# LoRA's output product one step later and in a bank of its own, and layer 1's k and v written as one 16-bit pair

## The reference, cut to what matters

```
x = x + tanh(g_xattn[0]) * L0_xattn(layernorm(x), ctx)   # 32 heads, 8 kv heads of 128, rms-normed q and k
x = x + tanh(g_ffn[0])   * L0_ffn(layernorm(x))          # LoRA experts behind a softmax router
x = x + tanh(g_xattn[1]) * L1_xattn(layernorm(x), ctx)   # 16 heads, 4 kv heads of 96, no norm of q and k
x = x + tanh(g_ffn[1])   * L1_ffn(layernorm(x))          # gated, 1792 wide

# L0_ffn
scores = H * softmax(x @ Wr.T + br)
low = einsum('bsd,hrd->bshr', x, A)
out = einsum('bshr,hor,bsh->bso', low, B, scores)        # H=8, r=16: 128 ranks
```

## Time and profile before

| | |
|---|---|
| median of 3 runs | 1188.02 us (1186.46 to 1189.14) |
| the profiled execution's own time | 1189.01 us |
| its span, first to last instruction | 1187.2 us |
| PE busy | 1129.7 us, 95% of the span |
| DVE busy | 844.7 us, 71% |
| ACT busy | 836.9 us, 70% |
| POOL busy | 374.2 us, 32% |
| mean granted clock of PE | 0.990 |

### The profile page before, as it was taken

One profiled execution on the slowest core, in us unless ns is written; L12 is line 12 of the kernel. 1 busy time (PEld: TensorE's weight loads), 2 busy tenths in 40 slices (PEclk: granted clock), 3 DMA queues, 4 the chain that ended last, 5 costly groups with the idle time before them and its releaser, 6 DMA issues.

```text
span 1187.2 us, 22719 instructions
## 1 busy us (share of the span) xinstructions
PE 1129.7 (95%) x7184; PEld 712.0 (60%) x7184; DVE 844.7 (71%) x2050; ACT 836.9 (70%) x2711; POOL 374.2 (32%) x685
## 2 busy tenths in 40 slices
PE   6789999999999999999999978799999999799998
PEld 4445666666666666666666645566676766455554
DVE  5578767767767767777677678988888888743434
ACT  5678878888888888878888677777777665522221
POOL 5554434334733333333343354321111121000000
PEclk9899999999999999999999999999999999999999
DMA  6465554464655545555545646758996796200000
GB/s 242 105 143 120 130 130 103 120 139 89 133 144 128 118 99 130 125 112 129 122 98 112 135 93 135 146 132 173 229 193 142 139 166 126 52 1 1 36 1 36
DMA packets 411991, 139.55 MB, mean 118 GB/s; under 512 B 386656, under 2 KB 396640, under 8 KB 411872
## 3 DMA queue, kind: packets, MB, share of 16 engines
q1 hardware_dynamic: 409968, 134.43, 51.2%
q0 software_dynamic: 1904, 3.67, 1.1%
HBM read 39.21 MB, written 2.10 MB: 35 GB/s over the span
## 4 chain that ended last, share of the span: by engine, by line
PE 79%; DVE 9%; ACT 5%; issue 3%; POOL 2%; DMA 1%; DVEq 0%; POOLq 0%; ACTq 0%
PE bank L519 22%; PE bank L520 22%; PE bank L521 22%; PE bank L720 8%; PE bank L739 4%; ACT probs L906 2%; DVE pieces L1084 2%; DVE stats L1095 1%; DVE mx L1185 1%; DVE x L1222 1%; ACT junk L811 1%; POOL rstd L1473 1%; DVE q_rows L1084 0%; DVE nb L1195 0%; DVE nb L1190 0%
## 5 line engine op out<-in xcount | busy, mean ns | idle before, releaser
L808 ACT ACTIVATE pieces<-probs,rs 128x256 f16<-128x256 f32 x384 | 166.3, 524 | 10.2 <-DVE rs L1202 9.4
L1185 DVE TENSOR_REDUCE mx<-bank 128x2 f32<-128x512 f32 x192 | 131.5, 685 | 56.8 <-PE bank L521 56.7
L1084 DVE SCALAR_TENSOR_TENSOR pieces<-probs,rs,pieces 128x256 f16<-128x256 f32 x384 | 163.3, 485 | 5.8 <-ACT pieces L808 5.0
L906 ACT ACTIVATE probs<-bank,nb,rq 128x256 f32<-128x256 f32 x256 | 141.1, 564 | 37.2 <-DVE nb L1190 36.9
L519 PE MATMUL bank<-wq,xT 128*128 128x512 f16 (+1 forms) x384 | 139.1, 362 | 2.7 <-DVE wq L1084 2.7
L519 PE MATMUL bank<-wo_hi,oT 128*128 128x512 f16 x352 | 133.4, 379 | 6.0 <-DVE oT L1084 4.6
L520 PE MATMUL bank<-wq,xT 128*128 128x512 f16 (+1 forms) x384 | 138.9, 362 | 0.0
L521 PE MATMUL bank<-wq,xT 128*128 128x512 f16 (+1 forms) x384 | 138.7, 361 | 0.0
L811 ACT ACTIVATE junk<-bank 128x128 bf16<-128x128 f32 x384 | 101.7, 289 | 52.0 <-PE bank L521 51.8
L521 PE MATMUL bank<-wo_hi,oT 128*128 128x512 f16 x352 | 133.4, 379 | 0.0
L520 PE MATMUL bank<-wo_lo,oT 128*128 128x512 f16 x352 | 133.4, 379 | 0.0
(11 more groups left out here) (187 smaller groups left out, 2651.2 us busy)
## 6 DMA issues: line engine op xcount, KB each, us to landing
raw_o<-in_wo_a SPq DMA_DIRECT2D x8, 1024.0 KB, 5.8
raw_q<-in_wq_a SPq DMA_DIRECT2D x7, 1024.0 KB, 5.9
raw_kv<-in_wkv_a SPq DMA_DIRECT2D x8, 512.0 KB, 3.8
turned<-pieces SPq DMA_TRANSPOSE x192, 2.8
raw_q<-in_wq_c SPq DMA_DIRECT2D x4, 768.0 KB, 5.0
raw_o<-in_wo_c SPq DMA_DIRECT2D x4, 768.0 KB, 5.1
down_rest<-in_down_t POOLq DMA_DIRECT2D x5, 512.0 KB, 4.3
ff_in<-in_gate_t SPq DMA_DIRECT2D x4, 448.0 KB, 4.0
```

The lines of the kernel that those rows point to most:

```text
L808: return act.activation(out, in_, ACT.Copy, scale=scale)
L906: act.activation(probs[:, h, :], bank[h // 2][:, (h % 2) * KV:(h % 2 + 1) * KV], ACT.Exp, bias=nb[:, h:h + 1], scale=scale, accum_out=sums ...
L1084: return dve.scalar_tensor_tensor(out, in_, scale, hi, ALU.mult, ALU.subtract)
L1185: dve.tensor_reduce(mx[:, pr], chunks(bank[i][:, :], 2), AX.X, ALU.max, negate=True).then_inc(mx_done, 1)
```

## The change

- LoRA's output product of tile t leaves step 59+t and stands in step 60+t behind the kv projection, in bank 3. PE's waits for `lora_added` ahead of the sums go; the product itself waits for the previous tile's.
- `lora_add` and the statistics of norm 2 go to the start of the next DVE step, behind `o_low`. In these steps the low pieces of the weights (`weight_low`) also go there, ahead of `lora_add`.
- Norm 2 is scaled by DVE (`norm_scale`, between the two row maxima) and copied to 16 bits by POOL, where ACT wrote both. POOL makes its rstd behind norm 1's rows, and no shift.
- In layer 1 ACT writes k and v as one 16-bit pair `kvp` (192 columns for each source) and DVE its low pieces; kn and POOL's k_pieces go, and k's transfer reads `kvp`. In layer 0 k_pieces writes into `kvp`.
- nb is a tensor_tensor in layer 0 and a tensor_scalar in layer 1. The tile `zeros`, its memset and a tile for `k_rows` go, `junk` shares memory with the feed-forward's hT, and one POOL wait is added at step 85.

```diff
-        v = [tuple(chunks(w, 2) for w in pair(f"v{i}", 2 * P)) for i in range(VS)]
+        kvp = [sb(f"kvp{i}", 8 * P, F16)[:, :].rearrange("p (j n d) -> p j n d", j=2, n=4) for i in range(VS)]
...
+        def kv_pair(n, c, i):
+            return kvp[n % VS][:, 1, 2 * c + i, :] if n < N0 else kvp[n % VS][:, :, 2 * c + i, 0:L1.hd]
...
+        def kv_source(n, i):
+            if n < N0:
+                return kv_bank(n)[:, i * L0.kvw + L0.hd:(i + 1) * L0.kvw]
+            return chunks(kv_bank(n)[:, i * L1.kvw:(i + 1) * L1.kvw], 2)
...
+        def low_late(n):
+            return beside(n + 1)[3] is not None
...
             def turn_k(n):
-                sp.wait_ge(klo_done, n + 1)
+                if n < N0:
+                    sp.wait_ge(klo_done, n + 1)
+                else:
+                    sp.wait_ge(vlo_done, 2 * n + 2)
                 if n >= 2:
                     sp.wait_ge(s_done, 2 * (n - 1))
-                sp.dma_start_transpose(k_half[n % 2], k_rows[:, :]).then_inc(kturned, 16)
+                if n >= 1:
+                    sp.wait_ge(kturned, 16 * n)
+                sp.dma_start_transpose(k_half[n % 2], kvp[n % VS][:, 0].rearrange("p n d -> p (n d)")).then_inc(kturned, 16)
...
             def lora_project_out(t):
                 pe.wait_ge(lora_lo, t + 1)
-                mm3(bank[2][:, :], tT[t % 2], lb, start=True, stop=True).then_inc(lora_out, 1)
+                if t >= 1:
+                    pe.wait_ge(lora_added, t)
+                mm3(bank[3][:, :], tT[t % 2], lb, start=True, stop=True).then_inc(lora_out, 1)
...
                 if T < N:
                     kv_proj(T)
-                if lora is not None and lora >= 1:
-                    pe.wait_ge(lora_added, lora)
-                if n == N0 + 3:
-                    pe.wait_ge(lora_added, NT)
+                if norm2 is not None:
+                    lora_project_out(norm2)
                 sums_of_step(n)
...
                 values(n)
-                if lora is not None:
-                    lora_project_out(lora)
...
-                    copy(v[n % VS][0][:, i, 0:L.hd], kv_bank(n)[:, i * L.kvw + L.hd:(i + 1) * L.kvw],
-                         alpha[:, i, c:c + 1]).then_inc(vhi_done, 1)
+                    copy(kv_pair(n, 0, i), kv_source(n, i), alpha[:, i, c:c + 1]).then_inc(vhi_done, 1)
...
-                if norm2 is not None:
-                    norm_scaled(2, norm2)
...
-                    dve.scalar_tensor_tensor(nb[:, pr], mx[:, pr], 1.0, rq[:, c:c + 2], ALU.mult, ALU.mult
-                                             ).then_inc(nb_done, 1)
+                    dve.tensor_tensor(nb[:, pr], mx[:, pr], rq[:, c:c + 2], ALU.mult).then_inc(nb_done, 1)
...
-                    dve.scalar_tensor_tensor(nb[:, pr], mx[:, pr], es[:, g % 2, s:s + 1], zeros[:, :], ALU.mult, ALU.add
-                                             ).then_inc(nb_done, 1)
+                    dve.tensor_scalar(nb[:, pr], mx[:, pr], es[:, g % 2, s:s + 1], None, ALU.mult).then_inc(nb_done, 1)
...
                 if n >= 1:
                     o_low(n - 1)
+                if n >= 1 and low_late(n - 1):
+                    for chunk in weight_chunks(n - 1):
+                        weight_low(*chunk)
+                if norm2 is not None:
+                    lora_add(norm2)
+                    norm_stats(2, norm2)
...
                 if S < N:
                     row_max(S, 0)
+                if norm2 is not None:
+                    norm_scale(2, norm2)
...
                 if T < N:
                     v_low(T)
+                if T < N0:
                     k_rows_scaled(T)
...
-                for chunk in weight_chunks(n):
-                    weight_low(*chunk)
-                if lora is not None:
-                    lora_add(lora)
-                    norm_stats(2, lora)
+                if not low_late(n):
+                    for chunk in weight_chunks(n):
+                        weight_low(*chunk)
...
-                if k in (1, 2):
+                if k == 1:
                     pool.wait_ge(norm[k].rstd, t + 1)
...
-                if k == 0:
+                if k in (0, 2):
                     pool.tensor_copy(rows[:, 0:D], xn[xn_slot(k, t)]).then_inc(norm[k].row_hi, 1)
...
-                if norm2 is not None:
-                    norm_rstd(2, norm2)
...
                 if norm2 is not None:
+                    norm_rstd(2, norm2)
                     norm_rows(2, norm2)
...
-                if T < N:
+                if T < N0:
                     k_pieces(T)
```

More of the change, by code:

```diff
@@ L189, in build @@
         xt = chunks(sb("x", NT * D)[:, :], NT)
-        junk = sb("junk", 6 * P, BF16)
         k_weight, q_weight = sb("k_weight", P)[:, :], sb("q_weight", P)[:, :]
         lora_act = [sb(f"lora_act{i}", P)[:, :] for i in range(2)]
+        junk = nc.alloc_sbuf_tensor_at("junk", [P, 6 * P], BF16, offset=(nc.sbuf_base + 31) // 32 * 32)
         hT = [tuple(sb(f"hT{i}_{w}", D, F32R)[:, :] for w in ("hi", "lo")) for i in range(2)]
@@ L241, in norm_bank, with v_piece, k_piece @@
             return bank[2 if k == 0 and t == 0 else 4 if k == 3 and t >= NT - 2 else 3]
+        def kv_pair(n, c, i):
+            return kvp[n % VS][:, 1, 2 * c + i, :] if n < N0 else kvp[n % VS][:, :, 2 * c + i, 0:L1.hd]
+        def v_piece(n, c, i):
+            return kvp[n % VS][:, 1, 2 * c + i, 0:layer_of(n).hd]
+        def k_piece(n, c):
+            return kvp[n % VS][:, 0, 2 * c:2 * c + 2, :]
+        def kv_source(n, i):
+            if n < N0:
+                return kv_bank(n)[:, i * L0.kvw + L0.hd:(i + 1) * L0.kvw]
+            return chunks(kv_bank(n)[:, i * L1.kvw:(i + 1) * L1.kvw], 2)
         def kv_bank(n):
@@ L551, in kv_proj @@
                 if n >= 2 and first:
-                    pe.wait_ge(kn_done, 2 * (n - 1) if n <= 4 else 2 * n)
+                    pe.wait_ge(kn_done if n <= N0 else vlo_done, 2 * (n - 1) if n <= 4 else 2 * n)
                 if t == 0 and first:
@@ L609, in values @@
                 for kt in range(2):
-                    last = mm3(bank[4][0:L.hd, :], [w[:, kt, 0:L.hd] for w in v[n % VS]],
+                    last = mm3(bank[4][0:L.hd, :], [v_piece(n, c, kt) for c in range(2)],
                                [turned_out[:, n % 2, c, kt] for c in range(2)], start=kt == 0, stop=kt == 1)
@@ L876, in v_hi @@
             def v_hi(n):
-                L, c = layer_of(n), set_of(n % NT)
+                c = set_of(n % NT)
                 act.wait_ge(kv_done, n + 1)
@@ L1100, in norm_scale @@
                 dve.wait_ge(norm[k].rstd, t + 1)
+                if k == 2 and t >= 1:
+                    dve.wait_ge(norm[k].row_lo, t)
                 if k in (0, 3) and t >= 2 and turned_by_dma(k, t - 2):
@@ L1152, in v_low @@
             def v_low(n):
[L1153 removed]
+                c = set_of(n % NT)
                 dve.wait_ge(vhi_done, 2 * n + 2)
                 for i in range(2):
[L1156 to L1157 removed]
+                    scaled_low(kv_pair(n, 1, i), kv_source(n, i), alpha[:, i, c:c + 1], kv_pair(n, 0, i)
+                               ).then_inc(vlo_done, 1)
             def k_rows_scaled(n):
[L1160 to L1162 removed]
+                dve.wait_ge(kr_done, n + 1)
                 if n >= 1:
@@ L1165, in k_rows_scaled @@
                 for i in range(2):
[L1166 to L1171, removed]
-                        dve.tensor_scalar(out, rows, alpha[:, i, s:s + 1], None, ALU.mult).then_inc(kn_done, 1)
+                    c = 2 * (n % 2) + i
+                    dve.scalar_tensor_tensor(kn[:, i * P:(i + 1) * P], kv_bank(n)[:, i * L0.kvw:i * L0.kvw + P],
+                                             kr[:, c:c + 1], k_weight, ALU.mult, ALU.mult).then_inc(kn_done, 1)
             def q_low(n):
@@ L1510, in k_pieces @@
                     pool.wait_ge(kturned, 16 * n)
-                rows = chunks(kn[:, 0:2 * L.hd], 2)
-                pool.tensor_copy(k_piece[:, 0, :, 0:L.hd], rows).then_inc(khi_done, 1)
+                rows = chunks(kn[:, :], 2)
+                pool.tensor_copy(k_piece(n, 0), rows).then_inc(khi_done, 1)
                 pool.wait_ge(khi_done, n + 1)
-                pool.tensor_tensor(k_piece[:, 1, :, 0:L.hd], rows, k_piece[:, 0, :, 0:L.hd], ALU.subtract
-                                   ).then_inc(klo_done, 1)
+                pool.tensor_tensor(k_piece(n, 1), rows, k_piece(n, 0), ALU.subtract).then_inc(klo_done, 1)
             def q_norm(n):
@@ L1652, in step @@
                     pool.wait_ge(kv_done, N - NT)
+                    pool.wait_ge(wq_done, KC * GROUPS)
                 if 85 <= n < 90:
@@ L1670, in _ @@
             pool.memset(both_half[:, 1:2], 0.5).then_inc(consts, 1)
-            pool.memset(zeros[:, :], 0.0).then_inc(consts, 1)
             pool.memset(kb[:, :], XS * XS * RMS_EPS * L0.hd).then_inc(consts, 1)
@@ L1674, in _ @@
             norm_rstd(0, 1)
-            pool.wait_ge(consts, 9)
+            pool.wait_ge(consts, 8)
             kv_scale(0)
```

6 lines of the change are left out of this document (1 added, 5 removed).

## The result

| | before | after |
|---|---|---|
| median of the runs | 1188.14 us (8 runs, 1186.46 to 1189.14) | 1192.76 us (8 runs, 1190.79 to 1197.73) |
| profiled execution, its span | 1189.01, 1187.2 us | 1193.52, 1191.4 us |
| ratio | | 1.0047, 95% interval 1.0029 to 1.0064 |

The change costs 4.6 us. The prediction was 1189.5 us (range 1183 to 1194), with "within 0.2%" as its likeliest case. The time lies in the range, but 0.4% above before it is outside that likeliest case and 0.8 us outside the author's own case (1187 to 1192). The runs of after also spread more than those of before.

What follows compares the result with a forecast made beforehand. TensorE was taken as full from step 69 on, and in layer 1's LoRA steps as waiting on the DVE, POOL and ACT loop. Terms -0.3+1.8+0.6+1.3-1.6-0.3 = +1.5 us on the 1188.0 median gave 1189.5 us, range 1183 to 1194.

Steps and rivals of the forecast that it cites:

- the author's own case: Whole kernel: the forecast's terms hold, 1187 to 1192 us around 1189.5; chance 0.42.
- The loop: LoRA rounds: xn waits for norm 2's rstd, second nb ends with POOL's subtraction at D+7.67, round 13.36 us.
- The sum: Whole kernel: all terms together +1.5 us against the profiled execution, 1190.5 against 1189.0 us.
- Step 60: Layer 0 projection beside LoRA: norm 2's subtraction on POOL ends slightly earlier, -0.3 us.
- Steps 61 to 64: Four LoRA rounds of 13.36 us, 53.4 against 51.6: +1.8 us; weight pieces pushing POOL's rstd and ACT's copies: +0.6.
- Steps 65 to 67: Last LoRA rounds: step 65 11.76 against 10.50 us, +1.3; steps 66 and 67 21.2 against 22.8 us, -1.6.
- Layer 1's pair: Layer 1's k and v pair: savings covered by busy TensorE; only the hold of sums_in in the tail goes, -0.3 us.
- nb's form: nb's other form in layer 0, covered by TensorE: 0 us.
- The first: LoRA rounds: POOL's new copy takes 0.95 or 1.12 us, not 0.65; slower, about 1193 us; chance 0.28.
- The second: LoRA rounds: DVE's work alone sets them, the wait for norm 2's rstd hidden; 1181 to 1184 us; chance 0.12.
- The third: LoRA rounds: second nb not held by POOL, 0.47 us saved in six rounds, 1186.7 us; chance 0.13.
- The fourth: Layer 1: k's transfer starts sooner and holes in its steps go, less than 1 us, 1188.7 us; chance 0.05.

Runs made afterwards that it cites:

- e1: The changed kernel with each of POOL's seven down-weight loads waiting for v's low part of its own step; 1190.38 us, ratio 1.0015.
- e9: e7 without the pacing of the seven down-weight loads; 1188.87 us, ratio 1.0001.
- e2: The kernel before, with all five late down-weight loads issued one behind another in step 85; 1198.74 us, ratio 1.0086.
- e10: The kernel before with only nb's new forms, tensor times tensor in layer 0 and tensor times scalar in layer 1; 1188.21 us, ratio 0.9998.
- e3: The changed kernel with the LoRA stage as before the change, layer 1's pair of k and v kept, the seven loads paced; 1188.29 us, ratio 0.9997.
- e7: e1 with POOL's root of norm 2 right behind norm 1's, and LoRA's add and norm 2's moments ahead of the weights' low parts; 1185.77 us, ratio 0.9978.
- e11: e7 without the pair: layer 1's k rows and k pieces as before, which pace the loads; 1189.56 us, ratio 1.0005.

## Why the prediction was right and wrong

- **The loop**: right, with one hold in another place. Its figures inside the round came out to 0.01 us (7.67 and 1.26 us, in step 65), xn's wait was 0.92 us for 0.9, and both nb ended with POOL's subtractions. The second nb took 0.27 to 0.28 us and not the 0.4 to 0.7 named as a sign, since lg lost 0.35 us to the cast ahead of it, which the forecast left out; the end is the subtraction's either way.
- **The sum without the burst** (e1): +1.8 us measured, +1.5 forecast, and that is near by luck in part. Up to tile 76 the forecast has +1.8 and e1's trace +2.9; the hole at tile 77, for which the forecast has nothing, gives 0.9 back.
- **Step 60**: 14.54 us against 14.68, -0.14 (forecast -0.3).
- **Steps 61 to 64**: +3.0 us against a forecast of +1.8 and +0.6. The two rounds of 13.4 are the forecast's 13.36. The two with two weight pieces are 0.55 longer: POOL's shift of norm 1, 0.26 us in step 65, takes 0.80 beside the weight piece,

```profile
732.77 0.80 POOL L1500 TENSOR_SCALAR shift<-moments,rstd 128x1 f32<-128x1 f32 x1
```

  and ACT's normalization begins as much later. I had bounded this term at 0.4 a round and taken 0.2 in three.
- **Steps 65 to 67**: from D = 758.94 to the last projection with norm 2 rows at 791.95, 33.0 us; forecast 11.76 + 21.2 = 33.0; before 33.3. The two terms apart were not right (12.8 and 20.2). The tail gained 0.6 us in after, from tile 91 on, where 0.3 was forecast.
- **Layer 1's pair "covered", "one queue wait at step 85: 0, covered by TensorE"**: this is the step that failed. I costed the pair's removal of a cast and a subtraction on POOL as POOL's idle time, and did not ask what stood behind them on that engine. What stood there were the down loads, in the same queue, paced only by those two instructions. The sign that it named, steps behind 69 unchanged at 8.5 us, is the one that failed: one of them took 13.03. The five loads were in the trace of before, one a step, each right behind a k piece, and the diff's `if T < N0: k_pieces(T)` stands a few lines ahead of them. Price by the runs: 2.4 to 3.8 us (e1), 2.7 to 3.1 (e9, the two earlier loads included in both), 10.2 in the kernel before (e2, the five loads alone).
- **nb's form**: 0, measured 0 (e10).
- **Rivals.** The first, slower by POOL's copy: fallen, the copy took 0.61 us, not 0.95; the 1193 that it gives is near the measured time by another cause. The second, DVE's work alone: fallen, since xn waits. The third, a gain of 0.47 us a round by an nb that is not held: fallen, though by another row than the one it was argued from; the second nb is held by only 0.05 us in layer 1, and the time went at lg. The fourth, that the pair acts in layer 1: there is a gain of 0.9 at tile 77 in after, e1, e3 and e7, though e11 without the pair has most of it too.
- The chance of a slower kernel was 0.36; the case that happened was not among the rivals, so that the range holds the time is luck.

The version that beats both is e7: the change, with POOL's root of norm 2 behind that of norm 1, LoRA's add ahead of the weights' low parts, and a wait that paces the loads. 1185.77 us, 0.9978 of before (0.9968 to 0.9988).

## What to carry to other kernels

When instructions leave an engine, list what is queued behind them there, DMA issues first: an instruction that costs nothing may be the only thing that paces the next. Give such a load its own wait on a counter that steps with the work. When a wait is moved and comes back under another name with the same size, the loop around it is what bounds; look in that loop for an engine that holds a small result (here a root of one column) behind a large operation it does not need.

## What the runs showed of the hardware

- Five loads of 512 KB on POOL's queue, issued within 3.63 us, delay the transposes on SP's queue that are issued among or behind them: 7.3 us from issue to landing instead of 2.9 behind one load in after, 5.6 in e9, 14.2 behind four in e2, though the rate moved was only 303 GB/s from 940 to 950 us. One load at a time, as in before and e1, left TensorE without a wait from 930 to 990 us.
- DVE's nb and lg<-lg,lrs, of 2 and 8 columns, were held to the end of a POOL cast or subtraction beside them: nb 1.07 us in before's form and 0.95 and 1.00 as tensor times scalar, instead of 0.22 to 0.23, and lg 0.59 us instead of 0.24. Not every small instruction is: the maximum lmx<-lg over 8 columns took 0.16 us in all eight rounds of after, at 735.38 inside a subtraction (735.30 to 736.46). POOL is held as well: its one-column shift took 0.80 us instead of 0.26 beside a DVE operation with two SBUF inputs. The Trainium skill (SBUF — State Buffer, SBUF: two separate sides) calls the pair of ports they share an exclusive lock, for whoever starts first and for the whole instruction; the ends of nb, lg and the shift agree.
- After a wait of 3 us TensorE's granted clock came back from 0.50 to 1.00 at different distances in kernels that stand there nearly equally long (3.23 us in before, 3.41 in e3): it was 0.50 until 775 us in e3 (rows above), and in before nearly full in the window from 771 us:

```profile
771.00:775.00 4.00, 4.00 (x44) 3.59 (x42) 2.24 (x9) 1.79 (x6) 1.00 (x3) 0.95 0.75 168
```

  The matmuls run at half speed from 769.70 to about 775.2 us in e3 and from 768.12 to about 771.3 in before. These 2.3 us more, at half speed, account for the 1.2 us by which e3's step is longer; why the clock came back later is not shown.
